# Eight experts written out one after another, with ScalarE's scaling of finished rows behind two layer slices and VectorE's adding of infinities at the end of a step

## The reference

```python
idx = argmax(softmax(h @ gate_w + gate_b)); prb = probs[idx]     # one of 8 experts per row
pos = place of the row among its expert's rows; kept = pos < 3125
buf[idx, pos] = h                                                 # (8, 3125, 256)
hmid = relu(einsum('ecd,edf->ecf', buf, w1) + b1)                 # 1024 hidden numbers
ybuf = einsum('ecf,efd->ecd', hmid, w2) + b2
y    = nan_to_num(ybuf[idx, pos] * prb * kept, posinf=1e4, neginf=-1e4)
x    = x + y
```

## Time and profile before

| what | us |
| --- | --- |
| median of three executions | 1583.46 (1578.39 to 1584.58) |
| the profiled execution | 1597.6 |
| its span, first to last instruction | 1595.8 |
| experts' blocks in it, first slice of block 0 to end of the last `y_sum` | 949.6 |

### The profile page before, as it was taken

The page is one execution under the profiler, slowest core; times in us unless marked ns, Lnnn a source line. Parts: engine busy times, 40 slices in busy tenths (PEclk is TensorE's granted clock), DMA queues, the critical chain, the costliest instruction groups (busy, mean ns, idle before and its releaser), DMA issues.

```text
span 1595.8 us, 26565 instructions
## 1 busy us (share of the span) xinstructions
PE 1283.3 (80%) x7955; PEld 1125.5 (71%) x7957; DVE 996.6 (62%) x2033; ACT 953.4 (60%) x2033; POOL 1001.0 (63%) x903
## 2 busy tenths in 40 slices
PE   2345699982399254999998999998999999998994
PEld 0223455551255144999998999898999999998994
DVE  7889799980489894655545455554545455545553
ACT  4888877860266302656656566665656576656663
POOL 7884788765467103666764766675766566665665
PEclk9967788986699655999999999999999999999997
DMA  9998654544686002422422332242423232222423
GB/s 336 283 353 285 162 84 65 77 50 50 149 274 212 0 9 77 96 41 42 99 44 44 84 45 42 40 96 40 96 43 46 43 93 40 44 44 36 96 38 45
DMA packets 131518, 153.35 MB, mean 96 GB/s; under 512 B 16640, under 2 KB 118208, under 8 KB 131328
## 3 DMA queue, kind: packets, MB, share of 16 engines
q0 software_dynamic: 50112, 62.49, 25.2%
q1 hardware_dynamic: 59696, 68.64, 13.3%
q10 hardware_dynamic: 21648, 21.58, 3.9%
HBM read 100.16 MB, written 52.49 MB: 96 GB/s over the span
## 4 chain that ended last, share of the span: by engine, by line
PE 37%; issue 8%; ACT 5%; POOL 3%; DVE 3%; another core or an unknown queue 3%; DMA 2%; ACTq 1%; DVEq 1%; POOLq 0%
PE f_ps_y L1443 19%; PE f_ps_h L1431 17%; ACT h_all L1370 2%; PE f_ps_x L1421 1%; ACT h_hi L1369 1%; DMA out<-clean,put_now 1%; POOL out L1321 1%; ACT f_xn L1354 1%; POOL sg L1307 1%; POOL xg L1303 1%; ACT y_all L1380 1%; DVE y_sum L1526 1%; DVE clean L1499 1%; DVE x_lo L1473 0%
## 5 line engine op out<-in xcount | busy, mean ns | idle before, releaser
L1443 PE MATMUL f_ps_y<-w_hi,h_hi 128*128 128x256 f32 x1200 | 342.4, 285 | 4.6 <-DVE h_lo L1478 3.5
L1443 PE MATMUL f_ps_y<-w_hi,h_lo 128*128 128x256 f32 x1200 | 338.0, 282 | 0.0
L1443 PE MATMUL f_ps_y<-w_lo,h_hi 128*128 128x256 f32 x1200 | 338.0, 282 | 0.0
L1303 POOL DMA_INDIRECT xg<-out,idx_now x153 | 183.2, 1197 | 246.5 <-issue 235.6
L1431 PE MATMUL f_ps_h<-x_hi,w_hi 128*128 128x384 f32 x800 | 281.0, 351 | 37.0 <-ACT h_all L1370 29.7
L1321 POOL DMA_INDIRECT out<-clean,put_now x153 | 245.4, 1604 | 52.4 <-issue 46.8
L1431 PE MATMUL f_ps_h<-x_lo,w_hi 128*128 128x384 f32 x800 | 273.7, 342 | 0.0
L1431 PE MATMUL f_ps_h<-x_hi,w_lo 128*128 128x384 f32 x800 | 273.3, 342 | 0.0
L1369 ACT ACTIVATE h_hi<-f_ps_h,c_b 128x384 fp32r<-128x384 f32 x400 | 240.2, 601 | 41.3 <-issue 16.8
L1380 ACT ACTIVATE y_all<-y_sum,prob 128x256 f32<-128x256 f32 x150 | 65.5, 499 | 313.2 <-DVE y_sum L1526 257.1
L1370 ACT ACTIVATE h_all<-f_ps_h,c_b 128x384 f32<-128x384 f32 x400 | 241.6, 604 | 0.0
(11 more groups left out here) (192 smaller groups left out, 2320.0 us busy)
## 6 DMA issues: line engine op xcount, KB each, us to landing
shared<-out SPq DMA_DIRECT2D x40, 512.0 KB, 4.0
w_raw<-in_w SPq DMA_DIRECT2D x18, 1024.0 KB
xin<-in_x SPq DMA_DIRECT2D x24, 512.0 KB, 7.4
out<-xin ACTq DMA_DIRECT2D x24, 512.0 KB
shared<-in_x SPq DMA_DIRECT2D x16, 512.0 KB
out<-shared ACTq DMA_DIRECT2D x16, 512.0 KB
dst_row<-in_dst SPq DMA_DIRECT2D x20, 256.0 KB
xg<-out,idx_now POOLq DMA_INDIRECT x153
```

Of the source, the lines that this page charges most:

```text
L1303: nc.gpsimd.indirect_dma_start(xg[:, i, :], None, out, bass.IndirectOffsetOnAxis(idx[:, i, 0:1].bitcast(U32), 0), bounds_check=ROWS - 1).t ...
L1443: ins = nc.tensor.matmul(ps_y[:, i], x[:, f, i * P:(i + 1) * P], weights[s][:, w], start=i != 1 and f == 0 and n == 0, stop=f == KF - 1 an ...
```

## The change

The loop over pairs is gone: on ScalarE, TensorE and VectorE the eight experts are written out in sequence, each with its own inner loop. The last expert splits nothing and its dummy load is gone. ScalarE scales the rows of block b - 1 in step b, behind `relu` of slices 0 and 1, instead of at the end of step b - 1; the last block's follow at the end. VectorE moves `next_prob` and `find_infinite` behind pair 0, and `add_infinities` and `keep_finite` behind `take_low`, ahead of the wait for TensorE.

```diff
 sync:
-            sp.wait_ge(hi_ready, CUTS * NEXP)
-            sp.wait_ge(lo_ready, CUTS * NEXP)
-            weights.load(sp, NEXP - 1)
             for n in range(2):
-                sp.wait_ge(weights.raw_in[n], 16 * (NEXP + 1))
+                sp.wait_ge(weights.raw_in[n], 16 * NEXP)
 scalar:
-            def step(e, b, split=None):
+            def step(e, b, split=None, behind=True):
                 for f in range(KF):
                     relu(e, b, f)
+                    if f == 1 and behind:
+                        scale_rows(b - 1)
...
                 take_high(b + 1)
-                scale_rows(b)
-
-            with act.Fori(0, NEXP // 2) as pair:
-                for s in range(2):
-                    e = 2 * pair + s
-                    start, end = bounds(act, e)
-                    step(e, start, (1 - s, 0))
-                    step(e, start + 1, (1 - s, 1))
-                    with act.Fori(start + 2, end) as b:
-                        step(e, b)
+
+            for e in range(NEXP):
+                start, end = bounds(act, e)
+                step(e, start, (1 - e % 2, 0) if e + 1 < NEXP else None, behind=e > 0)
+                step(e, start + 1, (1 - e % 2, 1) if e + 1 < NEXP else None)
+                with act.Fori(start + 2, end) as b:
+                    step(e, b)
+            scale_rows(end - 1)
 tensor (body of the block unchanged):
-            with pe.Fori(0, NEXP // 2) as pair:
-                for s in range(2):
-                    e = 2 * pair + s
-                    start, end = bounds(pe, e)
+            for e in range(NEXP):
+                s = e % 2
+                start, end = bounds(pe, e)
 vector:
             def step(e, b, split=None):
-                next_prob(b)
-                find_infinite(b - 1)
                 for j in range(KJ):
                     split_hidden(b, j)
+                    if j == 0:
+                        next_prob(b)
+                        find_infinite(b - 1)
                     if split is not None:
                         s, half = split
                         weights.split_low(v, tt, e + 1, s, half * KJ + j)
-                    if j == 0:
-                        add_infinities(b - 1)
-                    if j == 1:
-                        keep_finite(b - 1)
                 take_low(b + 1)
+                add_infinities(b - 1)
+                keep_finite(b - 1)
                 v.wait_ge(y_ready, b + 1)
                 tt(y_sum[:], ps_y[:, :BT], b2[:, bass.ds(e, 1)].broadcast_to([P, BT, D]),
                    ALU.add).then_inc(y_sum_ready, 1)
-            with v.Fori(0, NEXP // 2) as pair:
...
+            for e in range(NEXP):
+                start, end = bounds(v, e)
+                step(e, start, (1 - e % 2, 0) if e + 1 < NEXP else None)
+                step(e, start + 1, (1 - e % 2, 1) if e + 1 < NEXP else None)
+                with v.Fori(start + 2, end) as b:
+                    step(e, b)
```

More of the change, by code:

```diff
@@ L1448, in _ @@
             turn(0)
-            with pe.Fori(0, NEXP // 2) as pair:
-                for s in range(2):
-                    e = 2 * pair + s
-                    start, end = bounds(pe, e)
[L1453 to L1462, removed]
-                            if j == 0:
-                                turn(b + 1)
-                        ins.then_inc(y_ready, 1)
+            for e in range(NEXP):
+                s = e % 2
+                start, end = bounds(pe, e)
+                with pe.Fori(start, end) as b:
+                    pe.wait_ge(hi_ready, CUTS * e + CUTS)
+                    pe.wait_ge(lo_ready, CUTS * e + CUTS)
+                    pe.wait_ge(x_hi_ready, b + 1)
+                    pe.wait_ge(x_lo_ready, b + 1)
+                    for f in range(KF):
+                        up(b, s, f)
+                    pe.wait_ge(y_sum_ready, b + 1)
+                    for j in range(KJ):
+                        ins = down(b, s, j)
+                        if j == 0:
+                            turn(b + 1)
+                    ins.then_inc(y_ready, 1)
         @block.vector
```

## The result

The changed kernel takes **1539.59 us** (median of 4 runs, 1539.17 to 1541.6) where the kernel before takes 1582.55 (4 runs beside them): a ratio of 0.973 [0.970, 0.975], 43 us less. The forecast was 1573.6 in a range from 1556 to 1597: right in direction, far too small, and outside its range. In the later groups of runs four single executions took much longer than their neighbours (1635, 3964, 4254 and 4714 us); the medians are given with them, which moves none by more than 0.7 us, and the ratios and intervals are without them.

A forecast was written before the change was run, and what follows sets the result against it. TensorE was taken as the bound in the experts' blocks; -11.8 - 1.0 - 5.5 + 9 - 0.6 = -9.9 us, put on the median 1583.5, gave 1573.6 us, range 1556 to 1597.

The forecast's parts named there:

- the ceiling: Experts' blocks: some 64 us of TensorE's waits, restarts and lower clock are all that a change of order can win.
- part 3: VectorE's additions: moved, they no longer hold up `h_lo` of pair 1 behind the `put_now` wait; 5.5 us less.
- part 4: Inner blocks: scaling between slices 1 and 2 delays slice 6 where slice 0 is handed over late; 9 us more.
- Part 1: Three expert starts where the loop over pairs jumps back: writing out removes ScalarE's stall for code; 11.8 us less.
- Part 2: The other four expert starts lose bounds and the wait for `y_sum`, 1.0 us less; the eight second blocks unchanged.
- rival B: Inner blocks: ScalarE becomes the bound between slices 1 and 2, late hand-overs lock in; +14 us, 1598; chance 0.22.
- Part 5: Last expert: without eight high and eight low cuts and a 2 MB load, 0.6 us less.
- A: Inner blocks: fifteen pay in full for the moved scaling, second blocks 0.3 each; comes out even, 1581; chance 0.28.
- C: Inner loops written out straddle code pages and wait for code at each return on TensorE; +22 us, 1596; chance 0.03.
- D: Inner blocks: hand-overs prompt without the profiler, so the moved scaling costs nothing and more is won; 1556 to 1560; chance 0.13.
- no gap of 2 us at the starts: Sign at starts of experts: no gap of 2 us or more ahead of `h_hi` in the changed kernel's profile.
- first blocks at 19.5 to 21: Sign at the third, fifth and seventh expert: their first blocks take 19.5 to 21 us after the change.

The follow-up runs named there:

- second group: Runs on one chip beside the kernel before (1589.54 us): only the additions last 1550.22, all of VectorE's new order in the loops 1550.74, whole change 1541.81 us.
- extra-work pair: Kernel before with additions behind pair 2 and keeping behind pair 3, without and with two useless VectorE additions ahead of the wait for TensorE: 1576.2 and 1560.16 us.
- additions-last kernel: Kernel before with one edit, `add_infinities` and `keep_finite` moved to the end of VectorE's step: 1550.22 us (0.975), and 1551.11 us (0.973) on another chip.

## Why the prediction was wrong, point by point

**The bound** was read rightly: TensorE, at 17.65 to 17.70 us a block. So was the ceiling: some 64 us of the profiled execution, of which 60.4 went. What the forecast did not do was ask why so much of it should stay. Two of its steps failed, and they hang together: part 3, by far the larger, and part 4. Within the second group the whole change is 47.7 us against 9.9 forecast; of the 37.8 that are missing 33.8 are part 3's (39.3 against 5.5) and 9 are part 4's.

**Part 1, the jump back, -11.8:** right mechanism, about the right size. Together with ScalarE's order and the last expert's edit it is 8.9 us in the median, and 7.9 us at the three starts. That code had to be brought in is borne out by the times of the instruction queue's packets: after the branch at 835.50 one is moved at 837.44 to 837.76, ahead of the next instruction at 838.98. The forecast put the new blocks at 20.2; they take 18.0 (17.98 + 18.00 + 17.99 = 53.97 for the three), and the old ones take 20.3 to 21.5 when hand-overs are prompt, not 24: both ends were too high by the same late hand-overs. Not foreseen was that ScalarE's new order cures the jump within the loops. The Trainium skill, page "Runtime: NRT & Kernel Launch", section "Instruction fetch mechanics", says that a taken branch out of the window held stalls the sequencer and gives that as a reason to unroll. The stall is in the traces, as the earlier trace rows show; the advice was not needed here, since the loops with both orders run in 1540.67 us against 1539.79 written out.

**Part 2, other starts -1.0, second blocks 0:** they gave 82.59 - (125.81 - 53.97) = 10.8 and 6.4 us. With the additions last alone, these four starts take 71.55 us and the second blocks 141.75 on the other chip: both gains are of VectorE's edit, not of writing out.

**Part 3, VectorE's additions, -5.5: the step that failed.** This is the edit that matters, sized at an eighth to a seventh. Alone it gives 39.3 and 42.3 us on two chips. I counted the four waits that TensorE had for `h_lo` and stopped there. Two things were missing. First, the wait grows when the hand-overs become prompt: 15 to 28 us of `down` in the runs that kept it. Second, and larger, with the additions in VectorE's idle time the late hand-overs vanish: the gaps at slices 4 to 7 fall from 35.2 to 7.4 us in the second group, those in `down` from 5.8 to 0.3. The text said that they would lie in idle time; it took this for free, not for a gain.

**Part 4, scaling between slices 1 and 2, +9: failed with it.** It held the late hand-overs for something that stays and put their cause down to GpSimd's adds, which the change leaves where they are. It also counted too few: ScalarE's 15 waits gave about half of the inner blocks, while `y_sum` is late in 38 of all 50 blocks of the same trace. The adds do lie at the same place after, and the cost did not come: 1.2 us of gaps at slices 4 to 7 in all 50 blocks. The text said that the trace showed only a coincidence, and then argued on from it, rival B too. What the runs show in its place: take GpSimd's adds away, or give VectorE work ahead of `y_sum`, and most of the lateness goes (adds away: 8.4 us of gaps left; work given: 6.8, and 29.0 to 11.2 with the wait out of play). Why it goes is not shown. That scaling costs nothing where hand-overs are prompt is shown by the two kernels written out with and without it, 1556.72 and 1555.66 us; what it costs in a block with a late one, which is what the forecast priced, was never measured, since neither of them had such a block.

**Part 5** (the last expert's cuts and load, -0.6) was not measured by itself. The whole change in the second group is 47.7 us: 39.3 from the additions, -0.5 from the place of `find_infinite` (no difference), 8.9 from writing out, ScalarE's order and the last expert.

**The rivals.** A and B are out: no block pays for the scaling, since TensorE's gaps at slices 4 to 7 are 1.2 us in all 50 blocks. C: no inner loop shows a miss; TensorE is busy for all but 1 us of the stage. D had the right sign, "hand-overs are prompt", but put it down to the absence of the profiler, and without the term of part 3 it ended at 1556 to 1560. The range missed because no case had a moved instruction make another engine's hand-over prompt.

**The signs.** Right: no gap of 2 us at the starts, no `put_now` ahead of `h_lo`, TensorE's waits for `h_all` only six, at slice 6 and under 1 us each. Wrong: the third, fifth and seventh experts' first blocks at 19.5 to 21 (they take 18.0).

## What to carry to other kernels

An instruction that waits for a DMA to be written belongs behind all work that the bounding engine needs, and its price is not the few waits that the bounding engine shows: here these grew from 4 to 29 once other waits were gone. Where two things only coincide in a trace, don't let one be the cause in a sum: put useless work or a harmless substitute in its place and see whether the other stays. And compare on more than one chip, since here the same old kernel lay at 1571 to 1593 us on five occasions while the new one lay at 1540 and 1542 on two.

## What the runs showed of the hardware that was not expected

**TensorE's finished work is signalled to other engines late, by up to 2.9 us.** In block 5 of the kernel before, the last matmul of `down` and `y_sum` that reads it:

```profile
738.12 0.28 PE L1443 MATMUL f_ps_y<-w_hi,h_lo 128*128 128x256 f32 x1
...
739.31 1.62 POOL L1321 DMA_INDIRECT out<-clean,put_now  x1 [0.30 <-issue]
...
740.51 0.96 DVE L1526 TENSOR_TENSOR y_sum<-f_ps_y,b 128x768 f32<-128x768 f32 x1 [5.54 <-remote]
```

The matmul ends at 738.40, `y_sum` starts 2.11 us later. Nothing but this wait is in front of `y_sum`, and TensorE itself goes on with the next block at 738.41. It is the signal that comes late, not the waiting engine that wakes late. In the chain of waits the short piece ahead of `y_sum` starts when the semaphore is updated:

```profile
740.49 0.02 issue
740.51 0.97 DVE y_sum L1526
```

So it is in all late blocks of this profile: the trace has the update of `y_ready` 0.43 to 2.85 us after the end of the last matmul, and `y_sum` starts 0.02 to 0.14 us after the update. In a prompt block the update stands 0.01 us after that end. The three other profiles of the kernel before show the same. (The ends of matmuls in a profile are modelled; but prompt and late blocks are measured by the same model, and the next block's first matmul starts 0.12 to 0.13 us after the last one of `down` starts in both, within an expert.) ScalarE's slices come late in block 4 too. In the four profiles of the kernel before 31 to 38 of 50 blocks are late; with the additions or useless work ahead of the wait 0 to 3 are (13 with the useless work and the additions behind pairs 2 and 3). VectorE's idle time is not what sorts them. From kernel to kernel, 2.75 us gave none late on the first chip, 2.57 us gave 38 on the fourth, and 3.75 us without GpSimd's adds 16. From block to block, in the first profile of before, `y_sum` comes within 0.25 us in eight of the twelve blocks in which VectorE idled over 3.6 us, and comes 0.6 to 0.8 us late in eight of the twelve in which it idled under 1.9. **Open:** what delays the signal, why work on VectorE helps, and why chips differ. In the extra-work pair GpSimd's busy time rose too (600.11 to 656.61 us), so its own timing may be part of the path.

**Long waits can cost clock.** Of the starts of experts behind a jump back, in which TensorE has a gap of about 2 us or more, some were granted less than the full clock (25.28 us at 0.86, 21.49 at 0.92; 20.33 at 1.00), and so was one without a jump but with a gap of 2.75 us (22.24 us at 0.92). In three profiles of the kernel before and two of the additions-last kernel the clock fell to its lower level 13 times within the stage, each time beside a gap of 1.9 us or more; other gaps, of up to 2.6 us, cost none. After the change there is no such gap, and the whole stage runs at 1.00.

**The better versions are equal.** VectorE's order with the experts written out (1539.79 us), both orders in the loops (1540.67) and the whole change (1539.59 and 1541.81) can't be told apart, and TensorE is busy for 888 of the stage's 889 us: another order of the same matmuls has 1 us left to win. What would have to shrink is TensorE's own 17.65 us a block.
